# A linear-attention and feed-forward kernel: q in rows of 32 per head, and the sums of four heads by four row tiles

## The reference

```python
normed = rms_norm(x, gamma)
q, k, v = ...                       # 8 heads of 16, q scaled by 16 ** -0.5
q, k = second_taylor_expansion(q), second_taylor_expansion(k)
kv_state = einsum('bhnd,bhne->bhde', k, v)
den = einsum('bhnd,bhd->bhn', q, k.sum(axis=2))
out = einsum('bhnd,bhde->bhne', q, kv_state) / maximum(den, 1e-5)
x = layernorm(x + out.reshape(b, n, 128) @ w_out)
h = silu(x @ w1.T * s1) * (x @ w2.T * s2)      # 128 -> 512
h = gelu(h @ h1.T * hs1)                       # 512 -> 512
h = gelu(h @ h2.T * hs2)                       # 512 -> 512
x = layernorm(x + h @ w3.T * s3)               # 512 -> 128
```

## Time and profile before

| | |
|---|---|
| median of 3 runs | 576.32 us (576.15 to 576.57) |
| the profiled execution | 576.77 us |
| its span, first to last instruction | 575.0 us |
| granted clock of TensorE, mean | 0.983 |
| DVE busy | 458.6 us |
| ACT busy | 463.2 us |
| POOL busy | 164.4 us |

### The profile page before, as it was taken

One profiled execution on the slowest core, in us unless ns is written; L12 is line 12 of the kernel. 1 busy time (PEld: TensorE's weight loads), 2 busy tenths in 40 slices (PEclk: granted clock), 3 DMA queues, 4 the chain that ended last, 5 costly groups with the idle time before them and its releaser, 6 DMA issues.

```text
span 575.0 us, 11379 instructions
## 1 busy us (share of the span) xinstructions
PE 548.1 (95%) x3598; PEld 408.4 (71%) x3598; DVE 458.6 (80%) x976; ACT 463.2 (81%) x954; POOL 164.4 (29%) x246
## 2 busy tenths in 40 slices
PE   6869999999999999999999999999999999999994
PEld 3445877778687777768777776877777787786672
DVE  4775869878797988879798887979788797968664
ACT  4956797988879788887978888797888879787773
POOL 4541412323151332315133222413322241320000
PEclk9968999999999999999999999999999999999998
DMA  8000000000000000000000000000000000000000
GB/s 285 2 21 1 19 2 17 5 18 20 19 18 18 18 0 18 18 18 18 18 18 3 15 18 18 18 18 18 12 6 18 18 18 19 0 19 1 19 2 36
DMA packets 7366, 12.25 MB, mean 21 GB/s; under 512 B 816, under 2 KB 1840, under 8 KB 7344
## 3 DMA queue, kind: packets, MB, share of 16 engines
q1 hardware_dynamic: 7056, 11.86, 6.0%
q10 hardware_dynamic: 288, 0.10, 0.1%
HBM read 7.77 MB, written 4.19 MB: 21 GB/s over the span
## 4 chain that ended last, share of the span: by engine, by line
PE 69%; ACT 17%; issue 8%; DVE 5%; POOL 1%; DMA 1%; ACTq 0%; DVEq 0%; POOLq 0%
PE fps L422 20%; PE fps L423 20%; PE ring L359 6%; ACT phiT L644 5%; PE ring L389 5%; PE ring L339 4%; PE ring L313 4%; ACT fps L694 3%; ACT hid_hi L693 3%; PE ring L406 3%; PE ring L398 2%; PE ring L320 2%; ACT restq L649 2%; ACT x1T_hi L654 1%; PE fps L462 1%
## 5 line engine op out<-in xcount | busy, mean ns | idle before, releaser
L422 PE MATMUL fps<-hid_hi,w_hi 128*128 128x512 f32 x576 | 228.5, 397 | 2.3 <-DVE hid_lo L917 1.8
L423 PE MATMUL fps<-hid_lo,w_hi 128*128 128x512 f32 x576 | 226.9, 394 | 0.0
L422 PEld LDWEIGHTS fps<-hid_hi,w_hi 128*128 128x128 f32 x576 | 108.3, 188 | 29.3 <-DVE hid_lo L917 6.4
L693 ACT ACTIVATE hid_hi<-fps,col 128x512 fp32r<-128x512 f32 x128 | 90.5, 707 | 46.3 <-PE fps L423 45.9
L423 PEld LDWEIGHTS fps<-hid_lo,w_hi 128*128 128x128 f32 x576 | 108.4, 188 | 21.5
L917 DVE TENSOR_TENSOR hid_lo<-fps,hid_hi 128x512 fp32r<-128x512 f32 x128 | 88.1, 689 | 28.9 <-ACT fps L694 25.9
L644 ACT ACTIVATE phiT<-ring 128x512 f32<-128x512 f32 x128 | 78.6, 635 | 16.4 <-PE ring L339 16.2
L903 DVE SCALAR_TENSOR_TENSOR h<-fps,col,gate_zo 128x512 f32<-128x512 f32 x64 | 47.9, 748 | 49.8 <-ACT gate_zo L680 43.7
L694 ACT ACTIVATE fps<-fps,col 128x512 f32<-128x512 f32 x128 | 86.9, 679 | 0.0
L249 DVE TENSOR_TENSOR phi_k<-phi_k 128x896 f32<-128x896 f32 x64 | 73.0, 1145 | 1.4 <-ACT v_one L617 1.3
L339 PE MATMUL ring<-qT,sel 128*128 128x512 f32 x128 | 55.3, 441 | 7.7 <-ACT phiT L644 4.4
(11 more groups left out here) (98 smaller groups left out, 921.3 us busy)
## 6 DMA issues: line engine op xcount, KB each, us to landing
x_b<-in_x SPq DMA_DIRECT2D x16, 256.0 KB, 2.5
out<-gate_zo SPq DMA_DIRECT2D x16, 256.0 KB, 2.0
w_raw<-in_h SPq DMA_DIRECT2D x2, 1024.0 KB, 8.4
w_raw<-in_w SPq DMA_DIRECT2D x3, 256.0 KB, 4.0
sel_raw<-in_sel SPq DMA_DIRECT2D x1, 320.0 KB, 4.8
w_qkv_raw<-in_w_kv SPq DMA_DIRECT2D x1, 128.0 KB, 2.9
const<-in_consts ACTq DMA_DIRECT2D x1, 92.0 KB, 3.2
w_qkv_raw<-in_w_q SPq DMA_DIRECT2D x1, 64.0 KB, 2.9
```

Of the source, the lines that this page charges most:

```text
L422: nc.tensor.matmul(fps[:, bank, :], w_hi[:, o:o + P], hi, start=start, stop=False)
L423: return nc.tensor.matmul(fps[:, bank, :], w_hi[:, o:o + P], lo, start=False, stop=stop)
L693: nc.scalar.activation(hid[1 - layer][0][:, m, :], fps[:, bank, :], ACT.Gelu, scale=scale)
```

## The change

- q is projected in two tiles, qT0 and qT1. Each head has 32 rows, its 16 columns of w_q taken twice. ACT copies each whole tile as hi; `q_parts` on DVE computes hi * lo_rows + q, where lo_rows is 0 in the first 16 rows of a head and -1 in the other 16, so that, written in the rounded type, a head's 32 rows hold hi and lo.
- `sums_of_q(t, g)` makes four tiles at a time, each from the 32 rows of one head, with one 32 x 128 matrix of zeros and ones for each. It waits for q and for all four banks first.
- The order of RING, its banks, and the lists of PE, ACT, DVE and POOL change; project_kv 2 and 3 come earlier on PE, and the state goes into the middle of layer4.
- `product` waits for hi before its first matmul and for lo before its second.
- The fill (steps 0 to 2) is put in another order: ACT's sums of the weights' low bits, the rounding of the first weights (now on DVE), one square on DVE in step 0.

```diff
 RING = (
     ("stateT", MIDDLE, 0), ("restT", MIDDLE, 1), ("xT", FRONT, 2), ("acc0", MIDDLE, 0), ("acc1", MIDDLE, 1),
-    ("kv0", FRONT, 3), ("kv1", FRONT, 2), ("kv2", FRONT, 3), ("out", MIDDLE, 0), ("qT", FRONT, 1), ("kv3", FRONT, 2),
-    ("sq0", FRONT, 3), ("sq1", FRONT, 0), ("rest0", FRONT, 2), ("sq2", FRONT, 1), ("sq3", FRONT, 3), ("sq4", FRONT, 0),
-    ("rest1", FRONT, 2), ("sq5", FRONT, 0), ("state", FRONT, 1), ("sq6", FRONT, 3), ("sq7", FRONT, 2))
+    ("kv0", FRONT, 3), ("kv1", FRONT, 2), ("kv2", FRONT, 3), ("kv3", FRONT, 2), ("qT0", FRONT, 0), ("qT1", FRONT, 3),
+    ("out", MIDDLE, 1), ("sq0", FRONT, 2), ("sq1", FRONT, 1), ("sq2", FRONT, 0), ("sq3", FRONT, 3),
+    ("rest0", FRONT, 2), ("rest1", FRONT, 1), ("sq4", FRONT, 0), ("sq5", FRONT, 3), ("sq6", FRONT, 2),
+    ("sq7", FRONT, 1), ("state", FRONT, 0))
...
+            def sums_of_q(t, g):
+
+                if g == 0 and is_step(t, 0):
+                    pe.wait_ge(sel_ready, 1)
+                wait_q(t, g)
+                for l in range(4):
+                    bank_wait(RING, ring_free, t, f"sq{4 * g + l}")
+                for l in range(4):
+                    rows = slice(32 * l, 32 * l + 32)
+                    nc.tensor.matmul(ring[:, bank_of(RING, f"sq{4 * g + l}"), :], sel[rows, 0:P], qT[g][rows, :],
+                                     start=True, stop=True).then_inc(ring_full, 1)
...
+                nc.tensor.matmul(fps[:, bank, :], w[:, o:o + P], hi, start=start, stop=False)
+                if wait_lo is not None:
+                    pe.wait_ge(*wait_lo)
+                return nc.tensor.matmul(fps[:, bank, :], w[:, o:o + P], lo, start=False, stop=stop)
...
                     if m == 0 and made_by is None:
-                        pe.wait_ge(split_ready, KT * (t - 2) + k + 1)
+                        pe.wait_ge(hi_ready, KT * (t - 2) + k + 1)
+                        wait_lo = split_ready, KT * (t - 2) + k + 1
                     elif m == 0:
-                        pe.wait_ge(f_free[bank_of(FPS, f"{made_by}{k}")], read(FPS, t, f"{made_by}{k}"))
+                        pe.wait_ge(gelu_hi_ready, 2 * KT * (t - 2) + KT * ("two", "three").index(made_by) + k + 1)
+                        wait_lo = f_free[bank_of(FPS, f"{made_by}{k}")], read(FPS, t, f"{made_by}{k}")
...
+            def q_parts(t):
+
+                for g in range(2):
+                    bank = bank_of(RING, f"qT{g}")
+                    dve.wait_ge(q_hi_ready, 2 * t + g + 1)
+                    nc.vector.scalar_tensor_tensor(out=qT[g][:, :], in0=q_hi[g][:, :].bitcast(F32), scalar=lo_rows,
+                                                   in1=ring[:, bank, :], op0=ALU.mult, op1=ALU.add)\
+                        .then_inc(ring_free[bank], 1)
```

More of the change, by code:

```diff
@@ L141, in build @@
         k_mid = sb("k_mid", [P, 2, H, DH])
+        q_hi = [sb(f"q_hi{g}", [P, N], F32R) for g in range(2)]
         qT = [sb(f"qT{g}", [P, N], F32R) for g in range(2)]
@@ L321, in project_q, with wait_q @@
                                           start=(n == 0), stop=(n == 2))
                 mm.then_inc(ring_full, 1)
[L324 to L334, removed]
-                    pe.wait_ge(sel_ready, 1)
[L336 to L340, removed]
+            def wait_q(t, g):
+                pe.wait_ge(ring_free[bank_of(RING, f"qT{g}")], read(RING, t, f"qT{g}"))
@@ L517, in step @@
                     if ffn:
+                        layer3(t, 1, (0, 1, 2), in_full)
                         layer3(t, 0, (3,), in_full)
@@ L572, in second_step @@
                 apply_rest(1)
-                project_kv(1, 0)
-                project_kv(1, 1)
+                for j in range(NT):
+                    project_kv(1, j)
+                project_q(1, 0)
+                project_q(1, 1)
+                pe.wait_ge(w_out_loaded, 16)
+                project_out(1)
+                sums_of_q(1, 0)
                 pe.wait_ge(lo_sums_ready, 3)
@@ L711, in step @@
                 if middle:
-                    square_sums(t - 1, 7, 6)
-                if ffn:
+                    square_sums(t - 1, 5)
+                if ffn and not is_step(t, 2):
                     silu(t, 1)
@@ L752, in step @@
                 if is_step(t, 1):
-                    a, b = w_parts[0]
-                    nc.scalar.activation(w_hi[:, a:b], w_raw[:, a:b], ACT.Copy).then_inc(w_hi_ready[0], 1)
+                    weights_low_bits(2, 1)
+                if ffn:
+                    gelu(t, 0, 0)
+                    gelu(t, 0, 1)
+                if front and not is_step(t, 0):
+                    copy_q(t)
+                if is_step(t, 1):
+                    weights_low_bits(0, 2)
+                if ffn:
+                    gelu(t, 0, 2)
+                    gelu(t, 0, 3)
                 if front:
@@ L776, in step @@
                 if front:
+                    square_rest(t, 1)
+                if front and not is_step(t, 1):
                     square_sums(t, 4)
@@ L1132 @@
         _np.where(row < DH, 1.0, 0.5), (is_one | is_lin).T,
+        _np.where(row % 32 < DH, 0.0, -1.0),
     ], axis=1).astype(_np.float32)
-    of_head, e = row % 64 // DH, row % DH
+    e = row % DH
     pairs = (e == f % DH) | (e == (f + f // DH) % DH)
-    sums = [(of_head == hh) & pairs for hh in range(4)]
     eighth = (part < 8) & (e % 8 == part)
-    sums.append((of_head == f // 32) & (eighth | is_lin & (e == part - (LIN - MAIN))))
+    sums = [pairs, (row // 32 == f // 32) & (eighth | is_lin & (e == part - (LIN - MAIN)))]
     data["sel"] = _np.concatenate(sums, axis=1).astype(_np.float32)
```

193 lines of the change are left out of this document (80 added, 113 removed).

## The result

The changed kernel takes 639.19 us (median of 4 runs, 638.41 to 642.35), the kernel before beside it 576.45 (576.15 to 577.84): the ratio is 1.109, interval 1.105 to 1.114. The forecast was 633, the range 605 to 655. The profiled execution took 638.42 against 576.77: +61.65, where the sum had 56.8.

The account below looks back on a forecast made before the run. PE was taken to bound the kernel, with 32.97 us of work and 0.46 of waiting per 33.43 us step. 576.8 + 41 (wait) + 17 (clock) - 1.2 (tail) = 633.6, put at 633 us; range 605 to 655.

Parts of the forecast that it names:

- Place and size of the wait: PE's second group of sums waits some 3 us for ACT to square rest1: +2.97 a step, +41 us in all.
- the 0.21: On PE, the switch of form going into the state, counted in each step: 0.21 us.
- The clock: In the loop, PE's clock falls to 1.2 GHz after the wait in 10 of 14 steps, 1.7 us each: +17 us.
- Rival 1: In the loop the wait is there but PE's clock holds: 616 us; chance 0.25.
- The row tiles: On PE, a group of four row tiles for the sums runs side by side and costs 0.65 us.
- rival 2: On PE the row tiles run in turn, 0.6 us more for each of 28 groups, +17: 650 us; chance 0.08.
- The split waits: Hi and lo waits on PE gain nothing in the loop, but about one product at some four tail gaps: -1.2 us.
- The start: In the fill, q's later copy and sum against the filled gap before project_out, 1 to 3 us each: 0, with 3 either way.
- Rival 3: PE stays the bound if ACT gets from gelu(1,0) to rest1's end in under 4.1 us: 571 us; chance 0.07.

Follow-up runs that it names:

- e2: The changed kernel with ten unused products put on PE ahead of the second group of sums in steps 2 to 15; 619.21 us.
- e11: e10 with ACT's square of sq6 moved behind copy_y in the next step and the second group put behind layer4(0); 575.32 us, ratio 0.9964.
- e5: The kernel before with only the split waits added (hi before the first product, lo before the second); 576.15 us, ratio 0.9996.
- e4: The changed kernel with the old fill order for the low bits' sums: earlier reduction and branch, transpose_x1 right behind step 1's first group; 635.31 us.
- e8: e7 with unused products in PE's waits of steps 0 and 1 (6 and 7 ahead of step 0's groups, 15 behind project_out); 585.61 us.
- e6: e1 with, on PE, rest1 moved behind layer3(2: 2, 3) and the second group behind layer3(3: 2, 3); 591.56 us.
- e10: e8 with ACT's and PE's passes reordered, the next x's square moved to DVE and its sum ahead of gelu_tile(1,2); 581.1 us.
- e7: e6 with the fill order of e4; 587.55 us, ratio 1.0188.
- e1: The changed kernel with ACT's squares of both rests moved ahead of square(t+1), gelu(1,2) and x1_hi; 592.05 us.
- e3: The changed kernel with the second group of sums moved on PE behind layer3(3: 2, 3) and layer4(0, 1); 613.05 us.

## Why the prediction was right, and where it was off

- **Place and size of the wait:** right. Forecast: the second group behind ACT's square of rest1, an ACT chain of 7.15, gelu(1,0) 23.25 after layer 1's start, +2.97 a step. Measured: the line of 39.4 us in the table, a chain of 7.2, 23.06 (301.70 - 278.64), and +2.73 by e2. Part of the 0.24 is the switch into the state: the 0.21 was read behind a product that had waited, and in the changed kernel it is 0.10 (312.65 to 312.98, less 0.23). A small wait was not in the sum: rest1 on PE waits for the bank of sq1, 0.32 a step in the steps read (`PE ring L346` in the table). It costs nothing here, since PE waits for ACT behind it anyway.
- **The clock:** the mechanism was right, how often and how much were both off. Forecast: 10 falls of 1.7 us, 17 in all; measured: 13 falls, 18.9 in all by e2, some 1.45 each. Why none follows the wait in step 2 stays open. The fall lasts the 3.4 us that were read off. Rival 1 (the clock holds, 616) is what e2 brings about: 619.
- **Luck:** the wait was put 0.24 a step too high, the number of falls too low, and the two errors nearly cancel. That steps 2 to 15 came to 58.0 together, as forecast (41 + 17), says less than it seems.
- **The row tiles:** 0.65 was taken for a group, 0.63 measured; rival 2, tiles in turn, is out. PE's work in a step was put at 33.11; by e11 it is 32.94. The Trainium skill (TensorE: Matmul & The Clock Gate, Part 3, "Measured speedup vs the span model") has 3.07 for four row tiles; here four take 0.43 where four products take 0.92, which is 2.1, or 1.5 with the switches of form on either side (0.63), and this measurement is what counts here.
- **The split waits:** -1.2 was forecast for the tail; four gaps of one product each, as the forecast has them, are only 0.9. In e5's traces it is -0.8, and nothing that its median could tell. The tail of the changed kernel is 1.5 shorter; the reason for the rest stays open.
- **The start:** here a term was mis-sized. The step was "Both are of 1 to 3 us; I take 0, with 3 either way", for q's later copies and for the gap that they fill in step 1. It measured +5.1, outside the 3: the state of step 0 came 2.5 later and at the lower clock (4.31), the first group of step 1 waited 4.30 for q, and PE stood 3.24 at the branch. e4 gets 4.4 of this back by the order of the fill, e8 a further 2.7 by products in the waits (43.27 to 40.53). I had let the gap before project_out cover it and had not priced the clock of the fill, though the earlier trace rows show it. This is nearly all of the 4.85 by which the sum fell short.
- **Rival 3** (faster, if ACT gets through in time) named the right condition, and its time of 571 is not reached: with the waits nearly gone e11 is at 575. The forecast set 33.11 of work against a step of 33.43 that has a wait of 0.46 in it. Work against work, the tiles win next to nothing: 32.94 against 32.97, the three products more for q taken in. What could be won was the old wait, and in e11 one of 0.44 stands in its place.

## What to carry to other kernels

A group of tiles that starts together needs all its banks at once: look up what last held each bank, and place the group by the last of those readers, not by the first. The Trainium skill (TensorEngine Tiling (Array Packing), "PSUM Bottleneck") says that after a fourfold speedup of TensorE the emptying of PSUM may become the bottleneck. e6 agrees: PE's next wait, 1.09 at the state, is for ACT's reading of sq4's bank. In e10 one of the two waits left is of that kind (0.39, for copy_y), the other is for data (0.44, for hid_lo). When a wait is taken away, follow the engine that released it to where its unbroken row ends: as long as that row isn't shorter, the wait only moves to the next instruction that it feeds. Price a wait of PE together with the slower products behind it; here that added half as much again.

## What was not expected

- Useless work can pay: 140 products that nobody uses made a kernel 20 us faster (e2), 28 more in the fill were worth 5 us at the start of step 3 in the traces (e8 against e7) and 1.9 us by the medians.
- Between the fall in every step from step 3 on (the changed kernel) and none (e1) there is a state in which the clock falls in every other step, with the same program in each: 36.62, 35.07, 36.62 (e3).
- Where PE branches on a value that DVE has computed, it stands for 3.2 us in the changed kernel and 3.6 us in e1, with no semaphore that the profile shows as the reason. In the changed kernel one packet of 0.02 MB runs on a DMA queue for instructions (q8) in that time, at 42.8. In e4, where the branch stands ahead of the group's wait for q, PE has no such wait of its own, and that for q is no longer (3.96 against 4.30). So code that has to be fetched behind the branch is a likely reason, argued from its place and not tried.
